# A two-layer Mamba and expert kernel: its front stage in another form, with part of batch 1's front inside the first scan

## What is computed

```python
xs = clamp(layernorm(x_tokens)) ; xin, z = split(xs @ in_proj_w.T)     # 256 inner channels each
xc = conv1d(xin, conv_w, 4 taps, causal, one filter per channel)
xc = silu(xc + conv_b)
xdbl = xc @ x_proj_w.T                                                # 8 for dt, 16 for B, 16 for C
dt = softplus(xdbl[:, :8] @ dt_proj_w.T + dt_proj_b)
A = -exp(A_log)
h = exp(dt_t * A) * h + (dt_t * x_t) * B_t                            # for each token t, 16 states
y = sum_n(h * C_t) + xc * D
y = y * silu(z) ; out = layernorm(clamp(y @ out_proj_w.T))
```

## Time and profile before

| | |
|---|---|
| median of three runs | 220.72 us |
| the profiled execution | 221.12 us |
| its span | 219.3 us |
| mean granted TensorE clock | 0.958 |
| busy in the span | TensorE 84%, VectorE 66%, ScalarE 56%, GpSimd 50% |
| first input of the scan (line 700) begins | 35.27 us |
| last scan of batch 0 / of batch 1 (line 710) ends | 64.69 / 101.22 us |

### The profile page before, as it was taken

One profiled execution on the slowest core, in us unless ns is written; L12 is line 12 of the kernel. 1 busy time (PEld: TensorE's weight loads), 2 busy tenths in 40 slices (PEclk: granted clock), 3 DMA queues, 4 the chain that ended last, 5 costly groups with the idle time before them and its releaser, 6 DMA issues. The chain is left out here.

```text
span 219.3 us, 3893 instructions
## 1 busy us (share of the span) xinstructions
PE 184.9 (84%) x1224; PEld 152.1 (69%) x1224; DVE 144.9 (66%) x339; ACT 122.0 (56%) x279; POOL 109.0 (50%) x140
## 2 busy tenths in 40 slices
PE   4875697497688748579999999699999999999993
PEld 3864496243235313237899999699998899999992
DVE  1969794999999999995256482746237583343343
ACT  2015899476676445643467856567654656445530
POOL 5530534476766684639458445524445454444400
PEclk9999959979999997969999999999999999999998
DMA  6999960000000000000000000000000000000000
GB/s 164 348 338 321 321 182 0 0 3 0 0 0 3 0 0 0 0 0 0 4 0 0 3 1 0 3 0 0 3 1 0 3 1 3 0 25 3 1 0 24
DMA packets 6148, 9.64 MB, mean 44 GB/s; under 512 B 353, under 2 KB 2930, under 8 KB 6130
## 3 DMA queue, kind: packets, MB, share of 16 engines
q1 hardware_dynamic: 6130, 9.42, 14.2%
HBM read 9.15 MB, written 0.26 MB: 43 GB/s over the span
## 5 line engine op out<-in xcount | busy, mean ns | idle before, releaser
L844 DVE SCALAR_TENSOR_TENSOR acc<-dbx_ps,comb,acc 128x128 f32<-128x128 f32 x96 | 29.4, 345 | 35.9 <-PE dbx_ps L1097 34.6
L325 POOL TENSOR_TENSOR hc<-hs,cb 128x1024 f32<-128x1024 f32 x16 | 37.7, 2357 | 25.3 <-DVE hs L710 25.3
L1073 PE MATMUL bc_ps<-x_hi,w_hi 128*128 128x256 f32 x128 | 41.5, 324 | 0.0
L339 POOL TENSOR_TENSOR w_lo<-w1a,w_hi 128x256 fp32r<-128x256 f32 x32 | 23.8, 749 | 32.5 <-ACT w_hi L524 32.5
L532 ACT ACTIVATE hid<-bc_ps,par 128x256 f32<-128x256 f32 x64 | 26.8, 471 | 21.8 <-PE bc_ps L1075 21.7
L339 POOL TENSOR_TENSOR w_lo<-w1b,w_hi 128x256 fp32r<-128x256 f32 x32 | 23.8, 745 | 27.1 <-ACT w_hi L524 26.9
L710 DVE TENSOR_TENSOR_SCAN hs<-da,dbx_ps 128x1024 f32<-128x1024 f32 x16 | 36.5, 2279 | 0.1
L1075 PE MATMUL bc_ps<-x_hi,w_lo 128*128 128x256 f32 x128 | 36.0, 281 | 0.0
L1074 PE MATMUL bc_ps<-x_lo,w_hi 128*128 128x256 f32 x128 | 36.0, 281 | 0.0
L1097 PE MATMUL dbx_ps<-w2a,hid 128*128 128x128 f32 x256 | 34.1, 276 | 0.5 <-issue 0.3
L1097 PE MATMUL dbx_ps<-w2b,hid 128*128 128x128 f32 (+1 forms) x256 | 33.9, 276 | 0.5 <-DVE acc L844 0.5
(11 more groups left out here) (155 smaller groups left out, 242.9 us busy)
## 6 DMA issues: line engine op xcount, KB each, us to landing
w1a<-w_in SPq DMA_DIRECT2D x2, 1024.0 KB, 8.1
w1b<-w_in SPq DMA_DIRECT2D x2, 1024.0 KB, 12.3
par<-packed_in SPq DMA_DIRECT2D x1, 476.0 KB, 3.6
x_cm<-x_in SPq DMA_DIRECT2D x1, 256.0 KB, 2.9
y_out<-out_sb SPq DMA_DIRECT2D x2, 128.0 KB, 1.7
w2a<-w_in SPq DMA_DIRECT2D x2, 0.5 KB, 9.2
w2b<-w_in SPq DMA_DIRECT2D x2, 0.5 KB, 10.5
dtw<-dt_rows_in SPq DMA_DIRECT2D x1, 9.0 KB
```

What stands on the lines that cost most here:

```text
L325: nc.gpsimd.tensor_tensor(hc[p][:], hs[p][:], cb[p][:].rearrange("p i (o t) -> p i o t", o=1).to_broadcast([128, PAIR, DC, T]), ALU.mult). ...
L339: nc.gpsimd.tensor_tensor(w1_lo[p][:], w1[layer][:, bass.ds(u * UW, UW)], w1_hi[p][:].bitcast(F32), ALU.subtract).then_inc(s["w1_staged"], 1)
L844: nc.vector.scalar_tensor_tensor(acc[k][:, t, :], o_ps[:, w // span % RING, 128 * t:128 * (t + 1)], comb[layer][b][:, t, bass.ds(u, 1)], a ...
L1073: nc.tensor.matmul(h_ps[:, p, T * c:T * (c + 1)], w1_hi[w][:, at], x_hi[b][:], start=True, stop=False)
```

## The change

- The loads: x in two DMAs, one per batch, then a row with the dt bias and the taps, and small rows for the dt product; the packed parameters come after them.
- The convolution goes to TensorE: `rows_out` spreads the tap weights over the partitions by matmuls with ones, `taps` on VectorE multiplies them into in_proj's weight (four matrices per chunk), and `conv` is four matmuls per chunk on shifted windows of xs, which has four columns of zeros ahead of each batch. `conv1` does it for batch 1 during the first pairs.
- dt: x_proj's eight rows times dt_proj are multiplied beforehand into one 256 x 256 weight (`w_dt`), so that `v` is one product from xc; the bias comes from a matmul with one row.
- Silu is used as a function. It has a table of its own; a dummy Silu and dummy Lns (`logarithm_table`) stand ahead of waits.
- B and C are made token by token (`bc`), copied to `bc_tok`, and `rows` spreads one by transposes of a column that is read 128 times, four per spread.
- For batch 1, the convolution, Silu, z, B and C, the step size, its rounding and dtx are steps inside the pairs of batch 0's scan (`b1_in`, `b1_c`, `b1_out`). Its dtx is made by GpSimd behind the weighing of pair 6.
- There are four buffers of decays (AHEAD) instead of two. The first four weight splits move into the second scan (`stage`). The constants on VectorE and the halving of out_w on GpSimd are gone. The loops of the first scan are written out.

```diff
+        plan = [("constants",), ("x_stats", 0), ("x_stats", 1), ("rows_out",), ("x_norm", 0), ("taps", 0), ("inner_x", 0),
+                ("taps", 1), ("in_proj", 0), ("conv", 0), ("x_norm", 1), ("inner_x", 1), ("conv", 1), ("in_proj", 1),
+                ("v", 0), ("bc", 0), ("z", 0), ("softplus", 0), ("bc_copy", 0), ("z_copy",), ("first_rows",),
+                ("conv1", 0), ("second_b",), ("conv1", 1), ("second_c",)]
+        b1_in = {3: [("silu1",)], 4: [("bc_copy", 1)]}
+        b1_c = {1: [("conv1_copy",)], 5: [("softplus", 1)]}
+        b1_out = {1: [("z", 1)], 2: [("bc", 1)], 4: [("v", 1)], 5: [("rounding",), ("step_1",)], 6: [("step_x",)]}
         for k in range(NP):
+            plan += [("pair_in", 0, k)] + b1_in.get(k, []) + [("pair_c", 0, k)] + b1_c.get(k, [])
+            plan += [("pair_out", 0, k)] + b1_out.get(k, [])
+        for k in range(NP):
+            plan += [("pair_in", 1, k)] + [(name, 0, 0) for name in before_states.get(k, [])] + [("pair_c", 1, k)]
+            if k in (0, 2):
+                plan += [("stage", k), ("stage", k + 1)]
...
+            def step_1():
+
+                pool.wait_ge(s["rounded"], 1)
+                pool.wait_ge(s["ln_dt"], 2)
+                link(nc.gpsimd.tensor_tensor(dt_l[1][:], dt_l[1][:], dt_q[1][:], ALU.subtract))
+                nc.gpsimd.tensor_tensor(dt[:, :, 1, :], dt[:, :, 1, :], dt_l[1][:], ALU.add).then_inc(s["dt1_ready"], 1)
+
+            def step_x():
+                pool.wait_ge(s["dt1_ready"], 1)
+                nc.gpsimd.tensor_tensor(dtx[1][:], xc[:, :, 1, :], dt[:, :, 1, :], ALU.mult).then_inc(s["dtx_ready"], 1)
...
+            def logarithm_table():
+                link(nc.scalar.activation(scrap[:], ones[:, 0:1], ACT.Ln))
 
             def softplus(b):
 
+                if b == 0:
+                    logarithm_table()
                 act.wait_ge(s["dt_ps"], b + 1)
...
+                link(nc.scalar.activation(dt_a[b][:], halves(dt_ps[b]), ACT.Abs))
+                if b:
+                    nc.scalar.activation(dt[:, :, b, :], halves(dt_ps[b]), ACT.Relu)
+                nc.scalar.activation(dt_e[b][:], dt_a[b][:], ACT.Exp, scale=-1.0).then_inc(s["exp_dt"], 1)
+                act.wait_ge(s["exp_dt"], b + 1)
+                nc.scalar.activation(dt_l[b][:], dt_e[b][:], ACT.Ln, bias=ones[:, 0:1]).then_inc(s["ln_dt"], 1)
...
+            def silu1():
+
+                act.wait_ge(s["u1_ready"], 1)
+                nc.scalar.activation(xc[:, :, 1, :], u1[:], ACT.Silu).then_inc(s["xc_ready"], 1)
+                act.wait_ge(s["z_copied"], 1)
+                nc.scalar.activation(sz[:, :, 0, :], z0[:], ACT.Silu).then_inc(s["sz_ready"], 1)
+                act.wait_ge(s["z_ps"], 2)
+                nc.scalar.activation(sz[:, :, 1, :], halves(z_ps[1]), ACT.Silu).then_inc(s["sz_ready"], 1)
+                logarithm_table()
+
+            def decays(b, k, q):
+                m = k + NP * b
...
+                if m >= AHEAD:
+                    act.wait_ge(s["h_done"], m + (1 + RING - AHEAD))
...
+            def rounding():
+
+                dve.wait_ge(s["ln_dt"], 2)
+                link(nc.vector.tensor_scalar(halves(y_ps), dt_e[1][:], 1.0, 1.0, ALU.add, ALU.subtract))
+                nc.vector.tensor_tensor(dt_q[1][:], halves(y_ps), dt_e[1][:], ALU.subtract).then_inc(s["rounded"], 1)
...
+            def pair_in(b, k):
+                m = k + NP * b + 1
+                if 1 < m < NB * NP:
+                    inputs(m // NP, m % NP, m % RING)
+
+            def pair_out(b, k):
+                states(b, k, k % RING)
+                if b == 0 and k == 0:
+                    dve.wait_ge(s["bct_ready"], 1)
+                    dve.wait_ge(s["z_copied"], 1)
+                    inputs(0, 1, 1)
...
+            def tapped(bank, b, c):
+                for k in range(TAPS):
+                    ins = nc.tensor.matmul(bank, w_tap[:, c, k, :], xs[:, b, PAD - TAPS + 1 + k:PAD - TAPS + 1 + k + T],
+                                           start=(k == 0), stop=(k == TAPS - 1))
+                return ins
...
+            def v(b):
+
+                if b:
+                    pe.wait_ge(s["bct_ready"], 2)
+                    bias(b)
+                else:
+                    pe.wait_ge(s["wv_ready"], 1)
+                for c in range(DC):
+                    pe.wait_ge(s["xc_ready"], c + 1 if b == 0 else DC + 1)
+                    for j in range(DC):
+                        ins = nc.tensor.matmul(dt_ps[b][:, T * j:T * (j + 1)], w_dt[:, c, 128 * j:128 * (j + 1)], xc[:, c, b, :],
+                                               start=False, stop=(c == DC - 1 and j == DC - 1))
+                ins.then_inc(s["dt_ps"], 1)
...
             def rows(b, k, which):
 
                 for i in range(PAIR):
...
+                    n = k * PAIR + i + NS * which
+                    for t in range(TT):
+                        ins = nc.tensor.transpose(bc_ps[which][:, T * i + 128 * t:T * i + 128 * (t + 1)],
+                                                  bc_tok[:, b, t, n:n + 1].to_broadcast([128, 128]), ident[:])
                 return ins
```

## The result

The changed kernel took 230.62 us (median of four runs, 229.86 to 231.61) beside 220.41 for the kernel before in the same runs: the ratio is 1.048, with a 95% interval of 1.040 to 1.056. The profiled execution took 230.71 us. The forecast was 227.0 with a range to 231.0, so the sign was right and the loss too small by some 4 us: 6.3 were forecast, 10.2 came. The ratios in this document leave out executions that took over 1.5% longer than the fastest of the same kernel, while the medians take in all.

The account below looks back on a forecast made before the run. VectorE was taken to bound both scans. E(0) 30.7 + 24.2 + 2.5 + 1.6 + 7.2 + 3.9 = 70.1, stepwise 70.4, 5.7 later; 221.1 + 5.7 + 0.5 = 227.3, forecast 227.0 us, range 221.5 to 231.0.

Parts of the forecast that it names:

- E(7): E(k) is the end of VectorE's k-th scan; E(7) ends the first batch: forecast 70.4 us, 64.69 before.
- E(0): End of VectorE's first scan of the first batch: forecast 30.7 us, a gain of 9.8 over 40.47.
- another root 1.1, one scale 0.57, the transposes 0.44: Front, after the normalisation: steps in us towards xs at 11.6, a gain of 2.0.
- rival (2): Front and first scan: Ln's table also serves Exp, so E(0) is 28.3 and the time 223.4 us; chance 0.13.
- (a): First scan's start: second input made after E(0), rows for the third wait for TensorE; 2.5 us lost.
- rival (1): Low TensorE clock at 25 to 28 us doubles conv1: 229.3 us; chance 0.24 together with dear transposes.
- (c): First scan, ScalarE: a load, three Silus and the dummy Ln ahead of c rows 3; 1.6 us lost.
- (b): First scan, TensorE: rows by four transposes per spread, some 0.7 us; no cost by itself.
- (d): Batch 1's step size in the first scan: late `v`, VectorE idle 5.4 us at rounding; 7.2 us lost.
- (e): End of first scan: batch 1's dtx on GpSimd behind pair 6's weighing; VectorE idle 3.9 us.
- The rest after E(15): Experts, after the second scan: the stage keeps its length and starts when that scan is done.
- rival (3): First scan: batch 1's chain hides if `v` ends before 49 us; time 219.3 us; chance 0.13.

Follow-up runs that it names:

- e1: The changed kernel without the nine throwaway matmuls of `rows_out`; median 225.40 us, ratio 1.023.
- e2: e1 with the bias products made in `v`, where they are used; median 225.88 us, ratio 1.022.
- e10: e9 plus twelve throwaway matmuls on TensorE while it waits for batch 0's B/C copy; median 218.76 us, ratio 0.993.
- e12: e9 with both lots of batch 1's convolution moved ahead of `first_rows`; median 218.53 us, ratio 0.993.
- e11: The changed kernel with only `v` of batch 1 moved from pair 4 to pair 3; median 226.89 us, ratio 1.027.
- e6: The changed kernel with batch 1's whole chain inside the first scan one pair earlier; median 230.54 us, ratio 1.045.
- e8: e7 without both dummy Lns and with batch 1's rounding, sum and dtx in pair 5; median 226.62 us, ratio 1.026.
- e3: The changed kernel with batch 1's dtx one pair earlier, ahead of the weighing of pair 6; median 226.59 us, ratio 1.027.
- e9: e8 with batch 1's softplus back in pair 5; median 220.03 us, ratio 0.993.
- e4: The changed kernel with the step size's Lns replaced by Identity and both dummy Lns left out, so its output differs; median 226.64 us, ratio 1.026.
- e5: The changed kernel with the second half of batch 0's convolution ahead of batch 1's norms; median 226.85 us, ratio 1.028.
- e7: e6 with the edits of e1 and e5 added; median 225.78 us, ratio 1.025.

## Why the prediction came out as it did

**The frame held.** VectorE is the bound of both scans and E(7) carries over: E(7) missed the forecast by 3.4 us, and the execution's 230.71 missed 227.3 by the same. The differences add up so: E(0) +4.31, first scan -0.94, second scan -0.93, rest +0.95.

**The step that failed** is in the front: "another root 1.1, one scale 0.57, the transposes 0.44". The three instructions are priced rightly (the transposes took 0.44, the inner rows were even there at 9.32), but they were set one behind the other as if TensorE were free at 9.6, and so xs at 11.6. xs came at 16.64, 5.0 us later. It was busy until 15.3 with what the change puts ahead of `inner_x`, none of it in the sum:

| in TensorE's queue ahead of the transposes | us |
|---|---|
| tap weights spread (L889), two matmuls of four records | 3.78 |
| dt product (L893) | 1.91 |
| nine throwaway matmuls (L875) | 4.21 |
| bias for dt (L925) | 1.45 |

The prediction said that every engine runs the plan in order, and then, for these transposes, didn't look at TensorE's queue. The throwaway matmuls are the largest item (e1: E(0) -3.62), and the bias is behind them (e2: -0.71 more, a part of which can be the clock's, which rose 2.6 us sooner in e2 than in e1). With both gone, E(0) is 30.68 against 30.7 forecast. From xs to E(0) the chain took 18.4 us where 19.1 were worked out, so in sum nothing else in the front was missed. The queue cost this much in part because nearly all of it ran at TensorE's slow rate (see the last section); what it would cost at the fast rate was not measured. Two sums of the prediction aren't complete: the terms named for the front add up to 11.3, not 11.6, and the rival (2)'s E(0) of 28.3 comes without its working.

**The table loads** were placed rightly: Exp, Ln and the decays' Exp each pay 1.28 us, as the earlier trace rows showed, though the last was partly covered: the scan waited 0.84 us for the decays. The kernel after has 12 loads, the kernel before 4. The rival (2), that Ln's table serves Exp, is out; so the rule of the Trainium skill (ScalarE: Activation LUTs, Table sets) that one set holds both functions and spares the second load is not borne out by this kernel. (Which set a load brings, the trace doesn't show.) Nor is the drain that its section on what a load costs adds: Ln starts at 28.30, and its load ends at 28.28.

**(a)** was forecast at 2.5 us lost and cost 3.8 (E(1) - E(0) is 7.30). The difference of 1.3 is the rival (1), which did happen, with a chance of 0.24 on it; it had put 2.3 us on it. The granted clock, TensorE alone:

```profile
20.00:24.00 4.00, 3.78 (x20) 1.00 1.09 327
24.00:28.00 4.00, 1.87 (x13) 1.00 1.08 316
28.00:32.00 4.00, 2.82 (x11) 0.53 1.01 293
32.00:36.00 4.00, 4.00 (x15) 0.61 0.10 29
```

TensorE is idle for 3.31 us up to 29.18, waiting for the B/C copy; then the clock stands at its lower level, and the first lot of conv1 takes 3.62 us instead of 1.86. With the gap filled the lot takes 1.89 (e10), and ahead of the first rows both lots take 3.62 together (e12). Yet E(5) - E(0) is 21.53, on the forecast's 21.6, since the next term was too large by nearly as much.

**(c)**, ScalarE's Silus and loads ahead of c rows 3, was forecast at 1.6 and cost 0.43 (E(4) - E(3) is 3.88). The mechanism is the one named: ScalarE does the block from 42.51, the rows' spread waits 0.85 for its copy, and VectorE 0.46 for the rows. But c rows 3 were copied 5.3 us after E(1) where 5.9 were worked out, and the rows for input 5 were there 2.0 us behind that copy where 2.6 were worked out (the product took 0.98). So (c) was put 1.2 us too high and (a) 1.3 too low: that E(5) - E(0) is met is luck, an offset of two errors.

**(b)** was priced at nothing, and no pair without another cause is longer than 3.45 us (E(2), E(3) and E(5) each follow after 3.45). The four transposes of one spread took 0.65 in the kernel after (47.64), near the 0.7 assumed.

**(d)** was right in place, mechanism and size: 10.7 forecast and 10.13 measured for E(6) - E(5), VectorE idle 4.77 instead of 5.4, released by ScalarE's Ln. `v` with its bias starts 2.1 us before E(5), where the prediction had 1.1, and ends 0.9 behind it instead of 1.4. e11 shows it by one move (E(6) - E(5) 5.24), and e6 and e8 by failing.

**(e)** was right: 3.9 forecast, 3.69 measured, and e3 takes it away.

**The second scan** was forecast 0.5 longer for the weight splits on GpSimd; it is 0.43 shorter, 36.09 to 36.11 in eight of the thirteen kernels of the family. The mechanism is there, only smaller. Ahead of pair 2 the weighing follows straight upon the two splits (84.76 to 86.18 us), VectorE waits 0.23 us for the root behind it, and the pair takes 6.75 us instead of 6.53. What makes the scan shorter is its last pair, 2.50 us instead of 3.14, and it is TensorE's clock: the same sum, first in the kernel before (granted clock 0.62 from 96 to 99 us), then in the kernel after (1.00):

```profile
94.68 3.63 PE L977 MATMUL y_ps<-hc,ident 128*128 128x512 f32 x4 [2.57 <-POOL hc L325]
```

```profile
103.97 1.98 PE L986 MATMUL y_ps<-hc,ident 128*128 128x512 f32 x4 [2.36 <-POOL hc L326]
```

In e10, with the code of after there, the sum takes 3.68 at a granted clock of 0.57, and the scan 36.73. So this is chance between executions as well.

**The rest after E(15)** was assumed constant, and the code is. It took 0.95 us more in the profiled execution of after. The change does nothing there: kernels with the same code have 117.5 to 120.1.

**The range** ended at 231.0, at the measured level: 230.6 is the median, and the ratio applied to 220.72 gives 231.4. It left out a sum of bad cases, and TensorE's queue was not among the cases at all; that is why its upper end was too low. The rival (3) was rightly no more than a rival for this diff, though e9 shows what it needed: a whole pair between `v` and `softplus`, and dtx ahead of the weighing.

## What to carry to other kernels

When a step is timed by its own inputs, list for each engine that it passes through all that the diff queues ahead of it, the throwaway matmuls too: behind a wait that is already met they are plain delay. When a chain over three engines is laid into a software pipeline, what counts is the distance between producer and consumer in pairs, on each engine by itself; shifting the whole chain (e6) moves the stall, and shifting only the producer (e11) shortens it. And where an idle gap of TensorE stands ahead of a critical stretch, work that has to be done anyway fills it (e12) as well as throwaway work (e10): E(7) - E(0) is 30.94 and 30.90.

## What the runs showed of the chip

**TensorE is slow at the start of the execution, while its granted clock reads 1.00.** The throwaway matmuls of the kernel after, grouped by source line (min/median/max ns, first and last start):

```profile
L875 PE MATMUL dbx_ps<-ident x24: 421/421/582, 1.6 to 13.6; 128*128 128x128 f32 x24
```

In the kernel before, the transposes of the same shape between 11.7 and 13.2 us took 272 at the median. In e1 the first half of the convolution (12.80 to 16.58) ran at 0.47 us a record and the second, from 16.80, at 0.25, with a granted clock of 1.00 over the whole; at 0.50 in a later stretch records of this form take 0.45. So early on the durations are those of the lower level (1.2 GHz), whatever the view gives. The clock's own records in the kept traces say why: the first of them, a record of the upper level, begins at 9.5 us in the kernel before, 14.6 in the kernel after and 17.0 in e1, and ahead of it the view has nothing and gives 1.00. The Trainium skill (TensorE: Matmul & The Clock Gate, Seeing it yourself) warns that the clock's events in a trace are not always reliable; these rows agree. That first record, and the fast durations with it, comes at 12.8 to 22.4 us in the family (14.6, 21.9, 22.4, 12.8, 22.0 and 14.0 in after, e3, e4, e5, e6 and e11, with the throwaway matmuls of `rows_out`; 17.0, 14.4, 18.1, 16.0, 16.7, 17.6 and 16.1 in e1, e2, e7 to e10 and e12, without them). So it varies by 8 us (after and e11 against e3 and e6) with the same queue up to there, the throwaway matmuls don't settle it, and E(0) varies with it. What decides it was not tried further.

**The lower level comes around stretches with idle time and costs only where the path goes through TensorE.** In the kernel after it came in the gap of 3.31 us and showed in two stretches of 4 us each; in e9 it showed from 24 to 32 us, and in e10, with the gap filled, not at all in the front. A long gap isn't needed: in e5 the clock was at 0.57 from 16 to 20 us, with TensorE idle for no more than 0.96 us at a time from 8 us on. In e12 it lies at 28 to 36 (granted 0.71 and 0.50) and E(1) - E(0) is 5.81 all the same, since conv1 is done by then.

**The time after E(15) varies by up to 2.6 us between executions of identical code.** Where it is long, one stretch between the expert layers shows a lower granted clock. TensorE in the kernel after, and in the kernel before at the same distance from E(15):

```profile
148.65:168.65 20.00, 18.08 (x144) 0.91 0.00 1
```

```profile
140.00:160.00 20.00, 18.02 (x156) 1.00 0.01 2
```

As many us are busy, but 144 instructions are done instead of 156. The kernels whose rest is 119.0 or more (after, e2, e4, e12) show 0.91 in one such stretch; those with 117.5, and those with 118.1 to 118.3, show 1.00. In e9's runs the mean granted clock is 0.953 in all five of the group at 221 us and 0.961 or more in the other. This means that a gain of 1% in the front has to be read from E(k) or from many runs: e9, e10 and e12 beat the kernel before by the same 0.7%, with 6, 10 and 12 runs in the ratio. That the lower clock there makes all of the 2.6 us was not isolated.
